# Transposed scores of an attention block as two row tiles of 64, written into pairs of PSUM banks

## What is computed

```python
Q = rope(Q, freq)
K = rope(K, freq)
score = jnp.einsum('bhqd,bhkd->bhqk', Q, K) / scale
causal = jnp.tril(jnp.ones((1, 1, seq, seq), dtype=jnp.float32))
score = score - 10000000000.0 * (1.0 - causal)
score = score - jnp.max(score, axis=-1, keepdims=True)
weights = jax.nn.softmax(score, axis=-1)
attn = jnp.einsum('bhqk,bhkd->bhqd', weights, V)
```

## Time and profile before

| | before |
|---|---|
| median of 3 runs | 478.77 us (478.29 to 480.01) |
| profiled execution | 479.53 us |
| span of its core | 477.8 us |
| mean granted clock of PE | 0.955 |
| busy PE / PEld / DVE / ACT / POOL | 444.2 / 278.9 / 318.8 / 276.5 / 167.2 us |

### The profile page before, as it was taken

One profiled execution on the slowest core, in us unless ns is written; L12 is line 12 of the kernel. 1 busy time (PEld: TensorE's weight loads), 2 busy tenths in 40 slices (PEclk: granted clock), 3 DMA queues, 4 the chain that ended last, 5 costly groups with the idle time before them and its releaser, 6 DMA issues.

```text
span 477.8 us, 7339 instructions
## 1 busy us (share of the span) xinstructions
PE 444.2 (93%) x2340; PEld 278.9 (58%) x2340; DVE 318.8 (67%) x1059; ACT 276.5 (58%) x512; POOL 167.2 (35%) x167
## 2 busy tenths in 40 slices
PE   5877999999999999999999998989999999999991
PEld 2345555555545544545555544448887788788780
DVE  3889957777787787776867873314656756756753
ACT  1212056765766766757757656956566565665560
POOL 4514020240411502404205022026656555665661
PEclk9976579999999999999999999999999999999996
DMA  7977610312112303112122000000000000000000
GB/s 242 279 208 201 164 20 4 106 21 66 45 21 67 62 1 96 30 38 72 20 69 43 1 1 1 2 0 2 0 1 1 23 1 1 23 2 1 22 1 22
DMA packets 41749, 23.64 MB, mean 49 GB/s; under 512 B 31280, under 2 KB 33968, under 8 KB 41712
## 3 DMA queue, kind: packets, MB, share of 16 engines
q1 hardware_dynamic: 41712, 23.18, 17.8%
HBM read 14.26 MB, written 8.65 MB: 48 GB/s over the span
## 4 chain that ended last, share of the span: by engine, by line
PE 75%; DVE 8%; ACT 5%; DMA 5%; issue 4%; SPq 2%; POOL 0%; POOLq 0%; DVEq 0%; ACTq 0%
PE bank L968 16%; PE bank L984 16%; PE bank L1053 15%; PE bank L950 14%; PE bank L1064 7%; DVE maxima L718 3%; ACT num L545 3%; DVE num L777 2%; PE bank L1002 2%; PE bank L907 2%; DMA k_scratch<-rope_lo 2%; DVE num L850 2%; DMA q_scratch<-rope_lo 1%; ACT num L607 1%; SPq L325 1%
## 5 line engine op out<-in xcount | busy, mean ns | idle before, releaser
L545 ACT ACTIVATE num<-bank 128x512 f32<-128x512 f32 (+1 forms) x304 | 159.3, 579 | 98.4 <-PE bank L968 95.8
L950 PE MATMUL bank<-k_op,q_op 128*128 128x512 f32 (+15 forms) x384 | 126.9, 381 | 6.8 <-DMA q_op<-q_scratch 3.5
L968 PE MATMUL bank<-q_op,k_op 128*128 128x512 f32 (+1 forms) x304 | 129.8, 442 | 3.4 <-ACT num L545 2.3
L447 POOL TENSOR_SCALAR_AFFINE_SELECT num<-num 128x512 f32<-128x512 f32 x64 | 40.3, 636 | 214.1 <-ACT num L545 214.1
L718 DVE TENSOR_REDUCE maxima<-bank 128x1 f32<-128x512 f32 x128 | 87.7, 685 | 25.3 <-PE bank L950 24.6
L478 POOL TENSOR_TENSOR q_op<-num,q_op 128x512 fp32r<-128x512 f32 x64 | 82.9, 1299 | 60.4 <-ACT q_op L600 59.2
L950 PEld LDWEIGHTS bank<-k_op,q_op 128*128 128x128 f32 x384 | 76.0, 203 | 40.9 <-DVE maxima L718 23.0
L968 PEld LDWEIGHTS bank<-q_op,k_op 128*128 128x128 f32 x304 | 56.9, 191 | 65.1 <-ACT num L545 36.9
L984 PE MATMUL bank<-num,v_op 128*32 128x512 f32 (+3 forms) x768 | 82.5, 502 | 3.2 <-ACT num L545 2.5
L850 DVE TENSOR_TENSOR num<-bank,num 128x512 f32<-128x512 f32 x64 | 44.2, 691 | 56.9 <-ACT num L607 53.8
L1053 PE MATMUL bank<-q_op,w_hi 128*128 128x512 f32 x256 | 81.5, 400 | 0.4 <-DVE num L850 0.2
(11 more groups left out here) (87 smaller groups left out, 362.2 us busy)
## 6 DMA issues: line engine op xcount, KB each, us to landing
k_op<-k_scratch SPq DMA_DIRECT2D x16, 256.0 KB, 2.8
q_op<-q_scratch SPq DMA_DIRECT2D x64, 52.0 KB
w_raw<-in_w_all SPq DMA_DIRECT2D x6, 512.0 KB, 4.2
q_scratch<-rope_hi SPq DMA_DIRECT2D x8, 256.0 KB, 3.1
k_scratch<-rope_hi SPq DMA_DIRECT2D x8, 256.0 KB, 3.3
xT<-in_x_feat SPq DMA_DIRECT2D x4, 256.0 KB, 5.6
k_scratch<-k_op SPq DMA_DIRECT2D x2, 512.0 KB, 5.9
q_scratch<-rope_lo SPq DMA_DIRECT2D x4, 256.0 KB, 3.5
```

Of the source, the lines that this page charges most:

```text
L545: act.activation(num[:, t % PB, h:h + heads, off:CH], t_bank[k % TB][:, 0:heads * (CH - off)].rearrange("p (h t) -> p h t", h=heads), ACT. ...
L950: pe.matmul(s_bank[k % SB][:, 0:width], q_op[u][:, j, :, :].rearrange("p h q -> p (h q)"), k_op[u][:, lo:lo + width], start=True, stop=Tru ...
L968: pe.matmul(t_bank[k % TB][:, 0:heads * (CH - off)].rearrange("p (h j q) -> p h j q", h=heads, q=QD), k_op[w][:, kt * P:(kt + 1) * P], q_o ...
```

## The change

T becomes row-tiled. Each T unit is now two matmuls, one on the upper 64 rows of the array (heads 0 and 1) and one on the lower 64 rows (heads 2 and 3), `tile_position=(i * P // 2, 0)`. The two write into the two halves of a double bank, and one activation reads both halves, up to 1,024 elements a partition. A unit holds two heads where a head has 512 or 384 columns, and all four where it has 256 or 128. So a group has 20 units instead of 38, 40 T matmuls instead of 38, and 20 activations instead of 38. Two double banks take four of the eight banks, where T had three.

The banks for this come from S: S, MROWS and NORM now share one ring of three banks, in the order of the plan (`JOBS`), with one pair of semaphores, `job_ready` and `job_read`. In the last stage the small jobs keep `small_bank`. The constants of the plan are given anew for the bigger units. Four matmuls (`WARM`) whose result nobody reads stand before the first T of the prologue. The amounts of work for DVE, POOL, SP's DMAs, PV and the experts stay the same.

```diff
 def t_heads(c, kt):
 
-    return CH // (CH - t_off(c, kt))
+    return 2 if CH - t_off(c, kt) > CH // 2 else GH
...
-TB = 3
+TB = 2
...
+WARM = 4
...
-S_LATE, S_EARLY = 0, 3
-MROWS_AT, NORM_AT, MROWS0_AT, NORM0_AT = 5, 9, 18, 21
-PV_LAG, PV_LAG_LAST = 3, 6
+S_LATE, S_EARLY = 0, 2
+MROWS_AT, NORM_AT, MROWS0_AT, NORM0_AT = 2, 4, 9, 11
+PV_LAG, PV_LAG_LAST = 2, 3
...
+JOBS = [(s, step) for s, plan in enumerate(STAGES) for step in plan if step[0] in ("S", "MROWS", "NORM")]
+JOB = {x: i for i, x in enumerate(JOBS)}
...
+        low = [ps(f"bank{i}") for i in range(2)]
+        t_bank = [ps(f"t_bank{i}", 2) for i in range(TB)]
+        o_bank, small_bank = ps("o_bank"), ps("small_bank")
+        bank = [*low, *(t[:, i, :] for t in t_bank for i in range(2)), o_bank, small_bank]
+        job_bank = [low[0], low[1], small_bank]
+
+        def ring(s, step):
+
+            return small_bank if s == GROUPS else job_bank[JOB[s, step] % SB]
...
-                        act.activation(num[:, t % PB, h:h + heads, off:CH],
-                                       t_bank[k % TB][:, 0:heads * (CH - off)].rearrange("p (h t) -> p h t", h=heads),
+                        each = heads // 2
+                        act.activation(num[:, t % PB, :, off:CH].rearrange("p (i k) t -> p i k t", i=2)[:, :, h:h + each, :],
+                                       t_bank[k % TB][:, :, 0:each * (CH - off)]
+                                       .rearrange("p i (k t) -> p i k t", k=each),
                                        ACT.Exp, scale=scale).then_inc(t_exped, 1)
...
-                        pe.wait_ge(s_reduced, NS * s + k + 1)
-                        pe.matmul(s_bank[k % SB][:, 0:width], q_op[u][:, j, :, :].rearrange("p h q -> p (h q)"),
-                                  k_op[u][:, lo:lo + width], start=True, stop=True).then_inc(s_ready, 1)
+                        pe.wait_ge(job_read, JOB[s, step] + 1)
+                        pe.matmul(ring(s, step)[:, 0:width], q_op[u][:, j, :, :].rearrange("p h q -> p (h q)"),
+                                  k_op[u][:, lo:lo + width], start=True, stop=True).then_inc(job_ready, 1)
...
                     if plan is PROLOGUE and step == ("T", 0, 0, 0, 1):
                         pe.wait_ge(v_copied, CHUNKS)
+                        for i in range(WARM):
+                            pe.matmul(t_bank[0][:, i % 2, :], wqk[:, i % 2, :], xT[:, 0:CH], start=True, stop=True)
...
-                        pe.matmul(t_bank[k % TB][:, 0:heads * (CH - off)].rearrange("p (h j q) -> p h j q", h=heads, q=QD),
-                                  k_op[w][:, kt * P:(kt + 1) * P],
-                                  q_op[w][:, c * NB + off // QD:(c + 1) * NB, h:h + heads, :]
-                                  .rearrange("p j h q -> p h j q"), start=True, stop=True)\
-                            .then_inc(t_ready, 1)
+                        each = heads // 2
+                        for i in range(2):
+                            rows = slice(i * P // 2, (i + 1) * P // 2)
+                            head = 2 * i + h
+                            ins = pe.matmul(t_bank[k % TB][:, i, 0:each * (CH - off)]
+                                            .rearrange("p (h j q) -> p h j q", h=each, q=QD),
+                                            k_op[w][rows, kt * P:(kt + 1) * P],
+                                            q_op[w][rows, c * NB + off // QD:(c + 1) * NB, head:head + each, :]
+                                            .rearrange("p j h q -> p h j q"),
+                                            start=True, stop=True, tile_position=(i * P // 2, 0))
+                        ins.then_inc(t_ready, 1)
```

More of the change, by code:

```diff
@@ L62 @@
 SB = 3
-TB = 3
+TB = 2
 HB = 4
 PB = 3
+WARM = 4
 C_STEPS = 15
-C_AT = [4 + (7 * r) // 3 for r in range(C_STEPS)]
+C_AT = [2 + 16 * r // 14 for r in range(C_STEPS)]
 PROJ_FIRST = 6
@@ L148, with last_norm @@
 LAST = stage_plan(False, True)
-SMALL_0 = sum(x[0] in ("MROWS", "NORM") for x in PROLOGUE)
 SMALL = sum(x[0] in ("MROWS", "NORM") for x in STEADY)
+STAGES = [PROLOGUE] + [STEADY] * (GROUPS - 1) + [LAST]
+JOBS = [(s, step) for s, plan in enumerate(STAGES) for step in plan if step[0] in ("S", "MROWS", "NORM")]
+JOB = {x: i for i, x in enumerate(JOBS)}
+NJOBS = len(JOBS)
+LAST_JOBS = sum(s < GROUPS for s, _ in JOBS)
+def last_norm(s, c):
+    at = [JOB[x] for x in JOBS if x[1][:2] == ("NORM", c) and x[0] <= s
+          and (x[0] < s or STAGES[s].index(x[1]) < STAGES[s].index(("OCOPY", c)))]
+    return at[-1] + 1 if at else 0
 PIECE = 3 * E * F // (GROUPS - 2)
-assert NS % SB == 0 and NPV % PB == 0
+assert NPV % PB == 0
 W2_LAG = 3
@@ L179, in sem, with ps @@
             return ctx.enter_context(nc.semaphore(name))
-        bank = [ctx.enter_context(nc.psum_tensor(f"bank{i}", [P, CH], F32)) for i in range(8)]
-        s_bank, t_bank, o_bank, small_bank = bank[0:3], bank[3:6], bank[6], bank[7]
+        def ps(name, *banks):
+            return ctx.enter_context(nc.psum_tensor(name, [P, *banks, CH], F32))
+        low = [ps(f"bank{i}") for i in range(2)]
[5 more added lines that the diff above has]
+            return small_bank if s == GROUPS else job_bank[JOB[s, step] % SB]
         q_dram = nc.dram_tensor("q_scratch", (B * H, QROWS, S), F32).ap()
@@ L358, in _, with stage @@
             sp.dma_start(x_res[:, :, :], x_tok.rearrange("(t p) d -> p t d", p=P)).then_inc(ld_res, 16)
-            def stage(plan, s, u, small, load=False):
+            def stage(plan, s, u, load=False):
                 n = s - 1
@@ L368, in stage @@
                         to = u if (c == 0 or plan is PROLOGUE) else v
-                        sp.wait_ge(small_read, small + use + 1)
+                        sp.wait_ge(job_read, SB + JOB[s, step] + 1)
                         for h in range(GH):
@@ L388, in stage @@
                         load_k(s + 1, v, 1)
-            stage(PROLOGUE, 0, 0, 0)
-            for i in range(0, GROUPS // 2 - 1):
-                stage(STEADY, i * 2 + 1, 1, i * (2 * SMALL) + SMALL_0, load=True)
-                stage(STEADY, i * 2 + 2, 0, i * (2 * SMALL) + SMALL_0 + SMALL, load=True)
-            stage(STEADY, GROUPS - 1, 1, SMALL_0 + (GROUPS - 2) * SMALL)
-            stage(LAST, GROUPS, 0, SMALL_0 + (GROUPS - 1) * SMALL)
+            for s, plan in enumerate(STAGES):
+                stage(plan, s, s % 2, load=0 < s < GROUPS - 1)
             for ch in range(0, CHUNKS):
@@ L449, in stage @@
                             .then_inc(masked, 1)
-                    if split and step == ("T", 0, 0, GH - 1, 1):
+                    if split and step == ("T", 0, 0, 1, 1):
                         pool.wait_ge(w_hi_done, n + 1)
@@ L699, in split_max, with stage @@
                                          ALU.mult, ALU.subtract).then_inc(max_split, 1)
-            def stage(plan, s, chain, small):
+            def stage(plan, s, chain):
                 done = 0
@@ L730, in stage @@
                         _, c, use = step
-                        dve.wait_ge(small_ready, small + use + 1)
-                        dve.tensor_copy(max_rows[c][:, :], small_bank[0:2 * CH // QD, 0:P]).then_inc(small_read, 1)
+                        dve.wait_ge(job_ready, JOB[s, step] + 1)
+                        dve.tensor_copy(max_rows[c][:, :], ring(s, step)[0:2 * CH // QD, 0:P]).then_inc(job_read, 1)
                     if step[0] == "NORM":
@@ L927, in _, with stage @@
             pe.sem_inc(pv_done, PB)
-            def stage(plan, s, u, turn_u, turn_v, small):
+            def stage(plan, s, u, turn_u, turn_v):
                 n = s - 1
```

80 lines of the change are left out of this document (38 added, 42 removed).

## The result

| | before | after |
|---|---|---|
| median of 4 runs, us | 479.32 (478.29 to 480.01) | 495.88 (494.23 to 497.21) |
| profiled run, us (its span) | 479.53 (477.8) | 494.23 (492.5) |
| first T of the prologue starts at | 58.71 | 61.60 |
| end of the first stage | 94.92 | 99.79 |
| one steady stage, mean of six | 32.12 | 34.26 |

The account below looks back on a forecast made before the run. PE, busy 93% of the span, was taken as the bound. Steady stages 0, last stage -3, prologue 0 on 479.53 us, less 0.8 to the median: about 475.8 us; likeliest case 467 to 485, 8-in-10 range 448 to 490.

Parts of the forecast that it names:

- The prices of PE: Steady stage: matmul costs read from start-to-start distances on PE; 29.4 us of work before, T pairs -4.2, passages +5.6.
- a passage: On PE, each switch between full array and tiles: taken as 0.2 us, 28 more a steady stage, +5.6 us.
- Rival 1: On PE, passages between full array and row tiles cost little or nothing: stage 28.7, kernel about 451 us; chance 0.33.
- the term of the waits: Steady stage: PE's waits of 2.7 us fall to half, 1.4, with ends at 0.5 and 2.7.
- Rival 2: In T pairs, the two weight loads come one after the other: 2.2 us a stage, kernel about 492 us; chance 0.17.
- Rival 3: In the scores' ring, NORM and other small jobs hold S: at most 1.2 us a stage, inside the waits; no own chance.
- The last stage: Last stage, 27 us: four T banks for three, T -3.8, passages +2.0; -3 us taken, ends 0 and -6.
- WARM: Prologue: four extra matmuls last 1.9 us, 0.8 over the idle gap, may bring full clock forward; 0, ends -3 and +2.
- The experts: The experts' stretch: left as it is by the change, unchanged at 161 us.
- The sum of PE's own work: Steady stage without waits: 29.4 us, less 4.2 for T as pairs, plus 5.6 for passages.
- no different: Steady stage with work and waits summed: 32.2 us against 32.1, 31.3 to 33.5 by the ends of the waits.

Follow-up runs that it names:

- T two by two: Kernel before with the shared ring of three banks and every second T of a tile moved directly behind the first: 486.65 us, ratio 1.0162.
- the halves apart: Changed kernel with T over all 128 rows, no extra matmuls, and one S between the two matmuls of a T unit: 480.30 us, ratio 1.002.
- the shorter maxima: Unmasked maxima of S taken over the first half of their 512 columns only, in both kernels: changed kernel 480.94 us, kernel before 467.61 us.
- the kernel with fewer passages: Changed kernel with T units of a steady stage moved directly behind one another, 36 passages instead of 52: 505.95 us, ratio 1.0553.
- the kernel with late banks: Kernel before with five single T banks instead of three in the last stage, two of them idle S banks: 476.98 us, ratio 0.9957.

## Why the prediction was wrong

A steady stage, by what was changed (us; the difference of two kernels each):

| step | from | to | difference |
|---|---|---|---|
| S, MROWS, NORM in one ring of three | 32.12 | 32.76 | +0.65 |
| T two by two | 32.76 | 33.08 | +0.3 |
| T as double units, S in longer runs, new lags and places | 33.08 | 33.87 | +0.8 |
| row tiles | 33.87 | 34.26 | +0.4 |

**The prices of PE were right.** A pair takes the time of one, its loads lie side by side, and a passage costs 0.2 us, so the stage's 28 more passages and shorter T are the +1.4 us of the sum. The Trainium skill's "TensorEngine Tiling (Array Packing)", Key Properties, says that a change of the tiling mode drains the engine: the trace agrees for row tiles, with 0.09 us before the pair, 0.09 and a load of 0.11 behind it, and a load of 0.1 behind the matmul that follows. Rival 1, to which I gave 0.33, is refuted by the distance of 0.44 from pair to successor. The rule of the Trainium skill's "TensorE: Matmul & The Clock Gate", Part 3, The mechanism, that tiles at different rows run side by side, holds within the pair: its loads start 3 ns apart. It does not carry over the change of cut, where the 0.44 us stand.

**The step that failed is the term of the waits.** The text took "half of the present waits, 1.4, with ends at 0.5 and 2.7". They became 3.5 by the same ledger, beyond the upper end. The argument for half was that T would wait less for ACT. That part came true: 3.8 to 2.1 us. The next sentence named what stands against it (0.61 us of DVE for an S of 512, PE needs 0.23, four S in a row, three banks, now shared) and gave it no price. Its price was to be had from rows ahead of it. On three banks that DVE frees one by one, the fourth S of a run can't start before DVE has read the first. PE would like to start it some 0.6 us after the first (wide, narrow, wide: 0.24 + 0.12 + 0.24), and DVE is done with the first after 0.24 + 0.61, a bank still in use from the run before aside: a hold of about 0.3 us. Counted in the plan, with MROWS and NORM as members of the ring, before had three runs of three such jobs without T or PV between and none longer; after has five of three, three of four and one of six. As an estimate, the four runs that reach a fourth job are 1.2 us by 0.3 each, and all nine, if the bank is still in use from the run before, up to 2.7, on top of the 1.4 that remained. The upper end should have stood near 4 instead of at 2.7. That holds on a ring like this cost time is shown by the halves apart and by the shorter maxima; this count is an argument made afterwards. The 2.1 us a stage between forecast and result (34.26 against 32.2) are this term alone; seven times that is 14 us. The rest of the 20 us are 2.7 at the start, 0.6 less gained in the last stage, and 2.4 because the profiled run, from which the sum goes, stands above the median in before and below it in after.

**Rival 2** had the time right by luck: its reason is wrong, since the two loads don't follow one another. **Rival 3** was the right thought, mis-placed: 0.65 us a stage stands beside the waits, not inside them, 4.5 us over the kernel.

**The ends.** The last stage was forecast at -3 and came at -2.4, within its bounds. I had given two reasons, the banks and the T work less the passages. The first alone is enough for it; the second, as far as the estimate above goes, is masked by the fall of the clock, which the forecast of this stage did not have. WARM was forecast at 0 with ends -3 and +2, on a cost of 1.9 us: it cost 3.96 and brought a net loss of 1.2 to 1.6, within these ends. The error is in the duration: the plain float32 operands give two matmuls for each one in the program, each at 0.5 us. The experts were forecast unchanged and are within 0.6.

**Why the sign was lost.** The sum of PE's own work was +1.4 a stage from the start. The forecast of "no different" lived on waits that would shrink by as much, and the gain of 3 us on the last stage. Slower was left to rival 2 and a tenth of the chances, and the time over 485 to rival 2 alone, while the waits alone, at the value of before (2.7), would have given 33.5 and 485.

**Open.** Why the last 0.6 us of waits between the two kernels stay when DVE has 3.9 us less to do; how the 0.8 us of the third step divide between the double units and the new lags; and what lets the clock fall in steady stages of the kernel with fewer passages, while after keeps it until its last stage.

## What to carry to other kernels

When an edit packs one engine's matmuls into pairs, ask first what fills the space behind the pair: a consumer that needs 0.6 us for what PE makes in 0.24 evens out over a stage only as long as its jobs are spread, and here the order and the ring cost 1.75 us a stage where the tiling cost 0.4. Price a run on a ring from rows: what the consumer still has to read when the producer comes to the first bank again, times the number of such runs. And before paying for a denser form to relieve a stage that waits on a ring, give that ring the banks that lie idle there: this alone gained 2.3 us with a dozen lines.

## What the runs showed of the hardware

- A passage into or out of a pair of row tiles costs the same as one around column tiles, 0.2 us each: 0.09 at the change, and 0.11 of a load that shows behind the first matmul of the new cut. A pair's two weight loads start 3 ns apart and take 0.19 us together.
- The moment at which the clock rises in the prologue moves by some 3 us between profiled runs that have the same order of work up to there: at 66.1 us in before, at 69.0 in the kernel with late banks. The start of the first T moves too, 58.71 and 60.02, and the end of the first stage, 94.92 and 96.90. A difference of 2 us in the first stage of one profile is no result.
- With four plain float32 matmuls ahead of the first T the clock rose at 58.4 to 60.8 us in three of the four kernels that have them (in the fourth it had risen before they ran), against 64.6 to 69.9 in the nine without them. In three of the four it fell again behind that, in after from 65.3 to 68.7.
- The clock fell in the last stage of all four kernels with row tiles (in after from 307.6 to 311.0), twice in two of them, and in none of the nine others.
- In the kernel with the T together it fell at 175.1 in a steady stage, with PE busy 1.94 of the 2.00 us before, on S of 96 to 256 columns and the start of a PV.
